# One-hot matrices of the edge tiles on ScalarE instead of VectorE, in a graph network and expert kernel

## The chip, the core and the metric

The kernel runs on one core of a Trainium2 chip. The metric is the device time of one execution in microseconds (us). The core's engines are TensorE (PE in the rows, with PEld for the loading of its weights), VectorE (DVE), ScalarE (ACT), GpSimd (POOL) and SyncE (SP); they run side by side and wait for one another through semaphores. 16 DMA engines move data.

## What is computed

Two layers over 1,250 nodes of 1,024 features. The first is a graph layer with 8 relations and 21,250 edges; the second routes each node to 2 of 8 experts. Only the first matters here, and of it the sum over edges:

```python
u = x @ root + bias
for r in range(8):
    mask = (edge_type == r)
    sums = segment_sum(x[src] * mask[:, None], dst, num_segments=1250)
    cnt = segment_sum(mask, dst, num_segments=1250)
    u = u + (sums / maximum(cnt, 1)[:, None]) @ weight[r]
z = concatenate([u, x], axis=1) @ w_gate + b_gate
h = tanh(u) * z + x * (1 - z)
```

## The kernel before

The kernel first multiplies all nodes by each relation's matrix and stores the results in `Y`. It then takes, for every edge, the row of `Y` that belongs to its source and relation, weighs it by `edge_w` (one over the count), and adds it to its destination. Edges are sorted by destination into 184 tiles of 128 (`ET = 184`), each with destinations in one block of 128 nodes. The change lies in this edge stage.

The edge stage runs beside other products (`x @ root` and half of the gate's product). The generator `steps()` yields 320 "product" steps, of three matmuls each, and 184 "edges" steps, with one or two products between two edge tiles. TensorE, ScalarE and VectorE each walk through the same generator and issue their own part of each step, in that order; an engine's instructions run strictly in the order in which they are written here. "split" and "evacuate" steps belong to the products: halves of the next weights, and results copied from PSUM to `y_out`.

An edge tile t passes through these hands:
- GpSimd gathers 128 rows of `Y` by an indirect DMA into `gathered` (L1053), of which there are 5 buffers (`GR = 5`); it waits until tile t - 5 is used.
- ScalarE writes `ghi`, the row times its weight, rounded (L623, in `edges_hi`). It waits for the gather's landing and, since there are 3 `ghi` buffers (`HR = 3`), until tile t - 3 is used.
- VectorE writes the remainder `glo` (L942, in `edges_lo`), which waits for `ghi`.
- TensorE multiplies `ghi` and `glo` by the tile's one-hot matrix `sel`, four matmuls in all (L1211, L1212, in `edges`), and counts the tile in the semaphore `g_used` (edge_tiles_used).
- Every second tile VectorE adds two PSUM banks to `acc` (L952, in `accumulate`).

`sel` has row e and column d: 1 where edge e of the tile has destination d. It has room for 8 tiles (`SR = 8`) and is written for 4 at a time (`SG = 4`), called a set below: set n is for tiles 4n to 4n + 3. VectorE writes it in one comparison of `iota` (1 to 128) with `edge_dst` (1 to 128, out of that range for a padding edge) in `places` (L935). Sets 0 and 1 are written at the stage's start. Set m + 1 is written behind the work on tile 4m + 2, and may be written once tile 4m - 1 is used, which held its place before.

Of the kernel before, what the change touches and what calls it, by code (L numbers as in the profile page):

```python
# [5 lines left out]
F32 = mybir.dt.float32  # L6
# [4 lines left out]
ALU = mybir.AluOpType  # L11
ACT = mybir.ActivationFunctionType
AX = mybir.AxisListType

P = 128
# [31 lines left out]
def build_program(nc, x, src, dst, edge_type, weight, root, bias, w_gate, b_gate,  # L47
                  gate_w, w1, w2, w3, out):
    s = shapes(x, src, weight, w1, gate_w)
    N, D, R, X, H, NT, NP, KC, HC = (s[k] for k in ("N", "D", "R", "X", "H", "NT", "NP", "KC", "HC"))  # L50
    E, EFULL, EREST, ECOLS, ET, MT, MTE = (
        s[k] for k in ("E", "EFULL", "EREST", "ECOLS", "ET", "MT", "MTE"))
# [6 lines left out]
    with ExitStack() as ctx:  # L59
# [3 lines left out]
        def sem(name):  # L63
            return ctx.enter_context(nc.semaphore(name))
# [29 lines left out]
        iota = keep.put("iota", [P, 257], F32)  # L94
# [4 lines left out]
        edge_dst = keep.put("edge_dst", [P, ET], F32)  # L99
# [14 lines left out]
        R0 = R // 2  # L114
# [62 lines left out]
        tmp10 = z2t.put("tmp10", [P, 4, NT], F32)  # L177

        def x_tile(j):
            return x_first[:, j] if j < XA else x_last[:, j - XA]  # L180

        LN_GROUPS = ((0, 1), (1, 2), (2, 3), (3, 4), (4, 6), (6, 8), (8, NT))
# [5 lines left out]
            sem("ranks_done"), sem("ranks_read"))  # L188
        norm_ready, tr_done, hi_done, lo_done = (
            sem("norm_ready"), sem("transposed"), sem("xhi_written"), sem("xlo_written"))  # L190
        var_ready, sqrt_ready = sem("var_ready"), sem("sqrt_ready")

        groups = [list(range(a, min(a + 3, NT))) for a in range(0, NT, 3)]
        stage = nc.alloc_sbuf_tensor_at("w_stage", [P, 2, 2, HALF], F32, offset=OFF_STAGE)
# [80 lines left out]
        OUTS = 48  # L275
# [6 lines left out]
        row_moved = [sem(f"row_buffer_moved{i}") for i in range(5)]  # L282
# [19 lines left out]
        def w_rows(w, q, h):  # L302
# [5 lines left out]
        GR, HR, SR, SG = 5, 3, 8, 4  # L308
# [5 lines left out]
        sel = Zone(OFF_YOUT + 4 * KB, 4 * KB).put("sel", [P, SR, P], F32R)  # L314
# [7 lines left out]
        sel_ready, g_hi, g_lo, g_used, acc_done = (  # L322
            sem("sel_ready"), sem("rows_hi"), sem("rows_lo"), sem("edge_tiles_used"), sem("pairs_accumulated"))

        def steps():

            a, b = [(NT - 2, k) for k in range(KC)], [(NT - 1, k) for k in range(KC)]
            order = [(j, k) for j in range(NT - 2) for k in range(KC)] + a[:3]
            for k in range(3, KC):
                order += [b[k - 3], a[k]]
            order += b[KC - 3:]
            half, t, later = NT * KC, 0, {}
            for c in range(4 * half):
                g, (j, k) = c // half, order[c % half]
                yield "product", g, j, k

                if (c + 1 - LEAD) * ET // (4 * half - LEAD) > t:
                    yield "edges", t
                    t += 1
                if j == NT - 1 and k % 2 == 1 and g < 3:
                    later.setdefault(c + LAG_SPLIT, []).append(("split", g + 1, k // 2))
                if k == KC - 1:
                    later.setdefault(c + LAG_OUT, []).append(("evacuate", g, j))
                yield from later.pop(c, [])
            for c in sorted(later):
                yield from later[c]  # L350

        with nc.Block() as block:
# [134 lines left out]
            def _(act):  # L487
# [16 lines left out]
                def root_of(g):  # L504
                    a, b = LN_GROUPS[g]
                    act.wait_ge(var_ready, g + 1)
                    nc.scalar.activation(tmp10[:, 1, a:b], tmp10[:, 0, a:b], ACT.Sqrt).then_inc(sqrt_ready, 1)

                def x_hi(j):
                    for n in (2 * j, 2 * j + 1):  # L510
# [99 lines left out]
                def split_hi3(g, q):  # L610
                    act.wait_ge(w_in3[q % 2], 16 * (2 * (g - 1) + q // 2 + 1))

                    if q < 3:
                        act.wait_ge(w_free, 3 * (g - 1) + q + 1)
                    else:
                        act.wait_ge(y_ready3, g * NT)
                    nc.scalar.activation(whi3[:, 2 * q:2 * q + 2, :], stage[:, q % 2], ACT.Copy).then_inc(w_hi3, 1)

                def edges_hi(t):
                    act.wait_ge(g_in[t % GR], G0[t % GR] + 16 * (t // GR + 1))  # L620
                    if t >= HR:
                        act.wait_ge(g_used, t - HR + 1)
                    nc.scalar.activation(ghi[:, t % HR], gath[t % GR][:], ACT.Copy,  # L623
                                         scale=edge_w[:, t:t + 1]).then_inc(g_hi, 1)

                def evacuate3(g, j):
                    act.wait_ge(y_ready3, g * NT + j + 1)
                    if g * NT + j < 2:
                        act.wait_ge(row_moved[j], OUTS * (R - R0))
                    else:  # L630
                        act.wait_ge(y_out3[j % 2], 16 * (g * (NT // 2) + j // 2))
                    nc.scalar.activation(yout[:, j % 2], psum[j % 2][:], ACT.Copy).then_inc(y_evac3, 1)

                for what, *n in steps():
                    if what == "edges":
                        edges_hi(*n)
                    elif what == "split":
                        split_hi3(*n)
                    elif what == "evacuate":
                        evacuate3(*n)  # L640

            @block.vector
            def _(dve):
                v = nc.vector
# [95 lines left out]
                def normalize(g):  # L740
                    a, b = LN_GROUPS[g]
                    for j in range(a, b):
                        dve.wait_ge(xin[j], 16)
                        v.bn_stats(stat[:, j, 0, :], x_tile(j)[:, 0:HALF])
                        step1(v.bn_stats(stat[:, j, 1, :], x_tile(j)[:, HALF:D]))
                        step1(v.bn_aggr(aggr[:, j, :], stat[:, j, :, :].rearrange("p a b -> p (a b)")))
                    v.tensor_scalar(tmp10[:, 0, a:b], aggr[:, a:b, 1], EPS, None, ALU.add).then_inc(var_ready, 1)
                    step1(v.tensor_copy(mean[:, a:b], aggr[:, a:b, 0]))
                    dve.wait_ge(sqrt_ready, g + 1)
                    dve.wait_ge(var_ready, g + 1)  # L750

                    step1(v.reciprocal(tmp10[:, 2, a:b], tmp10[:, 1, a:b]))
                    step1(v.tensor_tensor(tmp10[:, 3, a:b], tmp10[:, 2, a:b], tmp10[:, 2, a:b], ALU.mult))
                    step1(v.tensor_tensor(tmp10[:, 3, a:b], tmp10[:, 3, a:b], tmp10[:, 0, a:b], ALU.mult))
                    step1(v.tensor_scalar(tmp10[:, 3, a:b], tmp10[:, 3, a:b], -0.5, 1.5, ALU.mult, ALU.add))
                    step1(v.tensor_tensor(rstd[:, a:b], tmp10[:, 3, a:b], tmp10[:, 2, a:b], ALU.mult))
                    for j in range(a, b):
                        v.tensor_scalar(x_tile(j), x_tile(j), mean[:, j:j + 1], rstd[:, j:j + 1],
                                        ALU.subtract, ALU.mult).then_inc(norm_ready, 1)
# [163 lines left out]
                v = nc.vector  # L923
# [3 lines left out]
                    v.tensor_tensor(wlo3[:, 2 * q:2 * q + 2, :], stage[:, q % 2],  # L927
                                    whi3[:, 2 * q:2 * q + 2, :].bitcast(F32), ALU.subtract).then_inc(w_lo3, 1)

                def places(n):  # L930

                    if SG * (n + 1) > SR:
                        dve.wait_ge(g_used, SG * (n + 1) - SR)
                    at = SG * n % SR
                    v.tensor_tensor(sel[:, at:at + SG],  # L935
                                    iota[:, 1:P + 1].unsqueeze(1).to_broadcast([P, SG, P]),
                                    edge_dst[:, SG * n:SG * (n + 1)].unsqueeze(2).to_broadcast([P, SG, P]),
                                    ALU.is_equal).then_inc(sel_ready, 1)

                def edges_lo(t):  # L940
                    dve.wait_ge(g_hi, t + 1)
                    v.scalar_tensor_tensor(glo[t % GR][:], gath[t % GR][:], edge_w[:, t:t + 1],  # L942
                                           ghi[:, t % HR].bitcast(F32), ALU.mult, ALU.subtract).then_inc(g_lo, 1)
# [9 lines left out]
                                    ALU.add).then_inc(acc_done, 1)  # L953

                dve.wait_ge(acc_set, NT - 1)
                for i in range(2, 4):
                    dve.wait_ge(row_moved[i], OUTS * (R - R0))
                places(0)
                places(1)
                for what, *n in steps():  # L960
                    if what == "edges":
                        t = n[0]
                        edges_lo(t)

                        if t >= HR and (t - HR) % GROUP == GROUP - 1:
                            accumulate((t - HR) // GROUP)
                        if t % SG == 2 and SR <= t + 2 < ET:
                            places((t + 2) // SG)
                    elif what == "split":
                        split_lo3(*n)  # L970
                for n in range((ET - HR) // GROUP, ET // GROUP):
# [1016 lines left out]
```

## Time and profile before

| | us |
|---|---|
| median of 3 runs | 1840.62 |
| lowest and highest run | 1838.92, 1841.84 |
| the profiled execution's own time | 1834.11 |
| its span, first to last instruction | 1832.4 |
| of it the edge stage, about 889 to 1310 | 421 |

The profile was taken from one further execution. Its times are counted from the span's start. A row's "idle before" is what an engine stood still ahead of the instruction, and the name behind it is what ended that; idle time of an engine that nobody waits for costs nothing.

### The profile page before, as it was taken

Reading aid. Unit: us, or ns where it says so; the run is one execution under the profiler, and the core shown is the slowest. Engines: PE = TensorE matmul, PEld = TensorE weight load, DVE = VectorE, ACT = ScalarE, POOL = GpSimd, SP = SyncE. Lnnn points to the kernel's source line nnn. Section 1 sums busy time; section 2 is a strip of 40 time slices with the busy share of each in tenths; the row PEclk is TensorE's granted clock in tenths of the full one; section 3 lists DMA queues with packets and bytes.
Section 4 is the critical chain, followed back from the end, with each engine's and each line's share of the span. In section 5 each row is a group of like instructions: output and inputs, shape, how many; then the busy total and the mean of one; then the engine's idle time right before and its main releaser. Section 6 shows DMA issues by size and latency. Waiting matters only on the chain. (4 is left out here: it accounts for less than half of the span.)

```text
span 1832.4 us, 22117 instructions
## 1 busy us (share of the span) xinstructions
PE 1708.7 (93%) x7873; PEld 1401.7 (76%) x7873; DVE 1096.1 (60%) x1444; ACT 727.0 (40%) x1230; POOL 749.1 (41%) x663
## 2 busy tenths in 40 slices
PE   7999999999999999999899999989789957999993
PEld 6888888888888888888687777767678846878882
DVE  8555556665464342424399998889799876334200
ACT  2316656631231313121256565556522103454551
POOL 1011222226775656302255545555265515455531
PEclk9999999999999999999899999999899968999997
DMA  5236555566224343434788888888745436877545
GB/s 204 92 121 224 169 176 178 161 193 199 87 92 156 115 152 114 148 127 143 245 281 297 266 283 277 265 290 273 263 170 171 149 115 218 227 186 208 138 88 150
DMA packets 141050, 339.69 MB, mean 185 GB/s; under 512 B 19332, under 2 KB 35764, under 8 KB 140864
## 3 DMA queue, kind: packets, MB, share of 16 engines
q0 software_dynamic: 50816, 159.29, 29.2%
q1 hardware_dynamic: 90128, 179.00, 29.1%
q8 instruction: 66, 1.08, 0.2%
q14 instruction: 40, 0.33, 0.1%
HBM read 241.19 MB, written 102.15 MB: 187 GB/s over the span
## 5 line engine op out<-in xcount | busy, mean ns | idle before, releaser
L1053 POOL DMA_INDIRECT gathered<-Y,edge_row x184 | 211.9, 1152 | 230.2 <-PE banks L1212 191.5
L623 ACT ACTIVATE ghi<-gathered,edge_w 128x1024 fp32r<-128x1024 f32 x184 | 211.7, 1152 | 171.7 <-DMA gathered<-Y,edge_row 162.0
L942 DVE SCALAR_TENSOR_TENSOR glo<-gathered,edge_w,ghi 128x1024 fp32r<-128x1024 f32 x184 | 232.2, 1282 | 48.3 <-ACT ghi L623 47.4
L1029 POOL DMA_INDIRECT edge_w<-INV,edge_key x184 | 207.9, 1130 | 116.8 <-DMA edge_w<-INV,edge_key 85.3
L1070 PE MATMUL banks<-whi,xhi 128*128 128x512 f32 x640 | 253.4, 396 | 0.4 <-DVE xlo L766 0.4
L1072 PE MATMUL banks<-whi,xlo 128*128 128x512 f32 x640 | 250.4, 391 | 0.0
L1071 PE MATMUL banks<-wlo,xhi 128*128 128x512 f32 x640 | 250.2, 391 | 0.0
L1211 PE MATMUL banks<-ghi,sel 128*128 128x512 f32 x368 | 149.0, 405 | 23.8 <-DVE glo L942 23.1
L573 ACT ACTIVATE ring_hi<-raw_chunk 128x512 fp32r<-128x512 f32 x112 | 66.5, 625 | 207.5 <-PE banks L1174 125.6
L1212 PE MATMUL banks<-glo,sel 128*128 128x512 f32 x368 | 144.5, 393 | 0.0
L1072 PEld LDWEIGHTS banks<-whi,xlo 128*128 128x128 f32 x640 | 120.6, 188 | 25.5
L1070 PEld LDWEIGHTS banks<-whi,xhi 128*128 128x128 f32 x640 | 120.9, 189 | 25.0 <-DVE xlo L766 0.8
L1071 PEld LDWEIGHTS banks<-wlo,xhi 128*128 128x128 f32 x640 | 120.9, 189 | 24.1
L1011 POOL DMA_DIRECT2D TW<-t_set x64 | 44.5, 742 | 218.0 <-DVE t_set L676 208.6
L1191 PE MATMUL banks<-whi,xhi 128*128 128x512 f32 x320 | 126.0, 394 | 3.2 <-DVE wlo L911 3.2
L502 ACT ACTIVATE y_out<-banks 128x512 f32<-128x512 f32 x80 | 47.3, 592 | 200.7 <-PE banks L1072 200.3
L1192 PE MATMUL banks<-wlo,xhi 128*128 128x512 f32 x320 | 125.8, 393 | 0.0
L1193 PE MATMUL banks<-whi,xlo 128*128 128x512 f32 x320 | 125.8, 393 | 0.0
L830 DVE TENSOR_TENSOR ring_lo<-raw_chunk,ring_hi 128x512 fp32r<-128x512 f32 x112 | 78.0, 698 | 78.7 <-ACT ring_hi L573 67.2
L1170 PE MATMUL banks<-ring_hi,xhi 128*128 128x512 f32 x320 | 124.6, 389 | 0.0
L1174 PE MATMUL banks<-ring_hi,xlo 128*128 128x512 f32 x320 | 124.6, 389 | 0.0
L1172 PE MATMUL banks<-ring_lo,xhi 128*128 128x512 f32 x320 | 124.6, 389 | 0.0
(316 smaller groups left out, 3677.6 us busy)
## 6 DMA issues: line engine op xcount, KB each, us to landing
raw<-in_L_ffn_w SPq DMA_DIRECT2D x24, 1024.0 KB, 10.2
Y<-y_out SPq DMA_DIRECT2D x80, 256.0 KB
t_set<-in_L_gnn_weight POOLq DMA_DIRECT2D x64, 256.0 KB
TW<-t_set POOLq DMA_DIRECT2D x64, 256.0 KB
raw_chunk<-TW SPq DMA_DIRECT2D x64, 256.0 KB
w_stage<-in_L_gnn_weight SPq DMA_DIRECT2D x30, 512.0 KB, 5.0
raw_chunk<-in_L_gnn_weight SPq DMA_DIRECT2D x48, 256.0 KB
Y<-half_v SPq DMA_DIRECT2D x40, 256.0 KB
```

The lines of the kernel that those rows point to most:

```text
L623: nc.scalar.activation(ghi[:, t % HR], gath[t % GR][:], ACT.Copy, scale=edge_w[:, t:t + 1]).then_inc(g_hi, 1)
L942: v.scalar_tensor_tensor(glo[t % GR][:], gath[t % GR][:], edge_w[:, t:t + 1], ghi[:, t % HR].bitcast(F32), ALU.mult, ALU.subtract).then_in ...
L1029: nc.gpsimd.indirect_dma_start(out=edge_w[:, t:t + 1], out_offset=None, in_=INV, in_offset=bass.IndirectOffsetOnAxis(ap=edge_key[:, t:t + ...
L1053: nc.gpsimd.indirect_dma_start(out=gath[t % GR][:], out_offset=None, in_=Y, in_offset=bass.IndirectOffsetOnAxis(ap=edge_row[:, t:t + 1], a ...
L1070: pe.matmul(psum[slot][:], xhi[:, k, at], whi[h][:, k], start=(k == 0), stop=False)
L1071: pe.matmul(psum[slot][:], xhi[:, k, at], wlo[h][:, k], start=False, stop=False)
L1072: ins = pe.matmul(psum[slot][:], xlo[:, k, at], whi[h][:, k], start=False, stop=(k == KC - 1))
L1191: pe.matmul(psum[j % 2][:], xhi[:, k, at], whi3[:, k], start=(k == 0), stop=False)
L1192: pe.matmul(psum[j % 2][:], xhi[:, k, at], wlo3[:, k], start=False, stop=False)
L1193: ins = pe.matmul(psum[j % 2][:], xlo[:, k, at], whi3[:, k], start=False, stop=(k == KC - 1))
L1211: pe.matmul(bank[:], sel[:, t % SR], ghi[:, t % HR, cols], start=start, stop=False)
L1212: ins = pe.matmul(bank[:], sel[:, t % SR], glo[t % GR][:, cols], start=False, stop=stop)
```

## The change

ScalarE makes `sel` in two passes. The first is `distances(n)`: four activations of 128x128, one a tile, each the absolute value of `edge_dst` less `iota`. `edge_dst` is a column with one value a partition and enters as the activation's bias. The second is `places(n)`: one activation of 128x512 over the whole set, the positive part (Relu) of 1 less the distance, with the 1 read from `iota` as bias. Distances are whole numbers, so the result is 1 at distance 0 and else 0. The semaphore that counted the square roots of the layer norm also counts the distances of a set, so that `places` starts on finished ones.

```diff
+                def distances(n):
+
+                    if SG * (n + 1) > SR:
+                        act.wait_ge(g_used, SG * (n + 1) - SR)
+                    for t in range(SG * n, SG * (n + 1)):
+                        ins = nc.scalar.activation(sel[:, t % SR], iota[:, 1:P + 1], ACT.Abs, scale=-1.0,
+                                                   bias=edge_dst[:, t:t + 1])
+                    ins.then_inc(sqrt_then_distance_ready, 1)
+
+                def places(n):
+                    act.wait_ge(sqrt_then_distance_ready, len(LN_GROUPS) + n + 1)
+                    at = SG * n % SR
+                    nc.scalar.activation(sel[:, at:at + SG], sel[:, at:at + SG].bitcast(F32), ACT.Relu, scale=-1.0,
+                                         bias=iota[:, 1:2]).then_inc(sel_ready, 1)
+
...
+                for i in range(2, 4):
+                    act.wait_ge(row_moved[i], OUTS * (R - R0))
+                distances(0)
+                distances(1)
+                places(0)
+                places(1)
                 for what, *n in steps():
                     if what == "edges":
                         edges_hi(*n)
+                        ahead, part = divmod(n[0] + SR - SG, SG)
+                        if n[0] >= SG and part == 0 and SG * ahead < ET:
+                            distances(ahead)
+                        if n[0] >= SG and part == 1 and SG * ahead < ET:
+                            places(ahead)
...
-                def places(n):
-
-                    if SG * (n + 1) > SR:
-                        dve.wait_ge(g_used, SG * (n + 1) - SR)
-                    at = SG * n % SR
-                    v.tensor_tensor(sel[:, at:at + SG],
-                                    iota[:, 1:P + 1].unsqueeze(1).to_broadcast([P, SG, P]),
-                                    edge_dst[:, SG * n:SG * (n + 1)].unsqueeze(2).to_broadcast([P, SG, P]),
-                                    ALU.is_equal).then_inc(sel_ready, 1)
-
...
                 dve.wait_ge(acc_set, NT - 1)
-                for i in range(2, 4):
-                    dve.wait_ge(row_moved[i], OUTS * (R - R0))
-                places(0)
-                places(1)
                 for what, *n in steps():
...
                         if t >= HR and (t - HR) % GROUP == GROUP - 1:
                             accumulate((t - HR) // GROUP)
-                        if t % SG == 2 and SR <= t + 2 < ET:
-                            places((t + 2) // SG)
```

On ScalarE, from tile 75 to tile 80 of the edge stage, stood before (the first `ghi` is tile 75's, the second tile 76's):

```order
L632 ACTIVATE y_out<-banks 128x512 [waits y3_stored0,y3_ready]
L623 ACTIVATE ghi<-gathered_135,edge_w 128x1024 [waits edge_tiles_used,pool_transfers_landed0]
L623 ACTIVATE ghi<-gathered_136,edge_w 128x1024 [waits edge_tiles_used,pool_transfers_landed1]
L623 ACTIVATE ghi<-gathered_137,edge_w 128x1024 [waits edge_tiles_used,pool_transfers_landed2]
L623 ACTIVATE ghi<-gathered_138,edge_w 128x1024 [waits edge_tiles_used,pool_transfers_landed3]
L632 ACTIVATE y_out<-banks 128x512 [waits y3_stored1,y3_ready]
L623 ACTIVATE ghi<-gathered_139,edge_w 128x1024 [waits edge_tiles_used,pool_transfers_landed4]
L623 ACTIVATE ghi<-gathered_135,edge_w 128x1024 [waits edge_tiles_used,pool_transfers_landed0]
```

In its place stands now, with L631 the distances of set 20, L638 its places and L647 the evacuation:

```order
L647 ACTIVATE y_out<-banks 128x512 [waits y3_stored0,y3_ready]
L623 ACTIVATE ghi<-gathered_135,edge_w 128x1024 [waits edge_tiles_used,pool_transfers_landed0]
L623 ACTIVATE ghi<-gathered_136,edge_w 128x1024 [waits edge_tiles_used,pool_transfers_landed1]
L631 ACTIVATE sel<-iota,edge_dst 128x128 [waits edge_tiles_used]
L631 ACTIVATE sel<-iota,edge_dst 128x128 x3
L623 ACTIVATE ghi<-gathered_137,edge_w 128x1024 [waits edge_tiles_used,pool_transfers_landed2]
L638 ACTIVATE sel<-sel,iota 128x512 [waits sqrt_then_distance_ready]
L623 ACTIVATE ghi<-gathered_138,edge_w 128x1024 [waits edge_tiles_used,pool_transfers_landed3]
L647 ACTIVATE y_out<-banks 128x512 [waits y3_stored1,y3_ready]
L623 ACTIVATE ghi<-gathered_139,edge_w 128x1024 [waits edge_tiles_used,pool_transfers_landed4]
L623 ACTIVATE ghi<-gathered_135,edge_w 128x1024 [waits edge_tiles_used,pool_transfers_landed0]
```

Four distances stand between the `ghi` of tile 76 and that of tile 77, the first with the wait for `g_used`, and the places between those of tiles 77 and 78. So the wait for tile 75 to be used, which VectorE had behind tile 78, ScalarE has behind tile 76.

On VectorE, from tile 78 on, stood before (L942 and `glo` are the remainders, L947 and the ISA rows read the block of the pair and wait, L952 adds):

```order
L942 SCALAR_TENSOR_TENSOR glo_143<-gathered_138,edge_w,ghi 128x1024 [waits rows_hi]
L947 TENSOR_LOAD tile_block
L947 ISA x2
L952 ISA [waits pairs_accumulated,edge_tiles_used]
L952 TENSOR_TENSOR acc<-acc,banks 128x1024
L935 TENSOR_TENSOR sel<-iota,edge_dst 128x512 [waits edge_tiles_used]
L942 SCALAR_TENSOR_TENSOR glo_144<-gathered_139,edge_w,ghi 128x1024 [waits rows_hi]
```

In its place stands now, L942 being L958, L947 L963 and L952 L968:

```order
L958 SCALAR_TENSOR_TENSOR glo_143<-gathered_138,edge_w,ghi 128x1024 [waits rows_hi]
L963 TENSOR_LOAD tile_block
L963 ISA x2
L968 ISA [waits pairs_accumulated,edge_tiles_used]
L968 TENSOR_TENSOR acc<-acc,banks 128x1024
L958 SCALAR_TENSOR_TENSOR glo_144<-gathered_139,edge_w,ghi 128x1024 [waits rows_hi]
```

The comparison between the addition and the remainder of tile 79 is gone; all else stands as it did.

## Rows read from the trace of the kernel before

**Rows 1.** The page's span and its busy times of the engines.
```profile
span 1832.4 us, 22117 instructions
...
PE 1708.7 (93%) x7873; PEld 1401.7 (76%) x7873; DVE 1096.1 (60%) x1444; ACT 727.0 (40%) x1230; POOL 749.1 (41%) x663
```

**Rows 2.** Busy time by stretch: the edge stage, and 50 us of it.
```profile
core 0: us, PE busy (x) PEld busy (x) DVE busy (x) ACT busy (x) POOL busy (x), PEclk, DMA share, GB/s
889.00:1310.00 421.00, 396.44 (x1675) 311.16 (x1674) 371.00 (x334) 241.36 (x236) 211.93 (x184) 0.99 0.85 279
950.00:1000.00 50.00, 47.76 (x200) 36.17 (x198) 46.52 (x43) 31.57 (x32) 25.69 (x23) 1.00 0.89 300
```

**Rows 3.** Who waited for whom, 889 to 1310 us: total, times, longest.
```profile
POOL gathered L1053 <- PE banks L1212: 191.5, 173, 7.1
ACT ghi L623 <- DMA gathered<-Y,edge_row: 162.0, 132, 8.9
...
PE banks L1211 <- DVE glo L942: 23.1, 26, 5.2
ACT ghi L623 <- PE banks L1212: 7.4, 6, 2.6
```

**Rows 4.** Instruction groups by line and form, 889 to 1310 us.
```profile
L942 DVE SCALAR_TENSOR_TENSOR glo<-gathered,edge_w,ghi 128x1024 fp32r<-128x1024 f32 x184 | 232.2, 1282 | 48.3 <-ACT ghi L623 47.4
L935 DVE TENSOR_TENSOR sel<-iota,edge_dst 128x512 fp32r<-128x512 f32 x46 | 31.5, 686 | 1.6 <-DMA Y<-half_u 1.6
```

**Rows 5.** ScalarE's groups by form, whole span.
```profile
L562 ACT ACTIVATE oh_val<-oh_val,val_dst 128x184 fp32r<-128x184 f32 x168 | 73.4, 437 | 41.4 <-DVE oh_val L659 41.4
...
L573 ACT ACTIVATE ring_hi<-raw_chunk 128x512 fp32r<-128x512 f32 x112 | 66.5, 625 | 207.5 <-PE banks L1174 125.6 <-DMA raw_chunk<-TW 36.0 <-issue 25.7
...
L494 ACT ACTIVATE whi<-w_stage 128x1024 fp32r<-128x1024 f32 x30 | 31.6, 1053 | 13.5 <-DMA w_stage<-in_L_gnn_weight 13.5
...
L507 ACT ACT_TABLE_LOAD x1 | 1.3, 1283 | 0.8 <-PEq L1978 0.8
...
L1675 ACT ACTIVATE pr<-lg 128x80 f32<-128x80 f32 x1 | 0.3, 269 | 4.5 <-DVE lg L1752 4.5
```

**Rows 6.** Timeline of ScalarE: activations back to back.
```profile
149.27 0.44 ACT L562 ACTIVATE oh_val<-oh_val,val_dst 128x184 fp32r<-128x184 f32 x1
149.61 0.43 ACT L563 ACTIVATE oh_val<-oh_val,val_src 128x184 fp32r<-128x184 f32 x1
```

**Rows 7.** Timeline, tiles 75 to 77: start, duration, instruction, idle before it.
```profile
1065.28 1.16 ACT L623 ACTIVATE ghi<-gathered,edge_w 128x1024 fp32r<-128x1024 f32 x1 [2.00 <-DMA gathered<-Y,edge_row]
...
1067.77 0.39 PE L1212 MATMUL banks<-glo,sel 128*128 128x512 f32 x1
...
1068.13 1.15 ACT L623 ACTIVATE ghi<-gathered,edge_w 128x1024 fp32r<-128x1024 f32 x1 [1.70 <-DMA gathered<-Y,edge_row]
...
1069.32 1.28 DVE L942 SCALAR_TENSOR_TENSOR glo<-gathered,edge_w,ghi 128x1024 fp32r<-128x1024 f32 x1 [0.22 <-ACT ghi L623]
...
1070.96 0.39 PE L1211 MATMUL banks<-ghi,sel 128*128 128x512 f32 x1
```

**Rows 8.** Timeline: the last matmul of tile 88, and ScalarE's tile 91 behind it.
```profile
1098.99 0.39 PE L1212 MATMUL banks<-glo,sel 128*128 128x512 f32 x1
1099.47 1.15 ACT L623 ACTIVATE ghi<-gathered,edge_w 128x1024 fp32r<-128x1024 f32 x1 [0.25 <-PE banks L1212]
```

**Rows 9.** Timeline of TensorE: tile 3's end, tile 5's start; tile 175's, tile 177's.
```profile
911.51 0.39 PE L1212 MATMUL banks<-glo,sel 128*128 128x512 f32 x1
...
914.99 0.47 PE L1211 MATMUL banks<-ghi,sel 128*128 128x512 f32 x1
...
1292.00 0.40 PE L1212 MATMUL banks<-glo,sel 128*128 128x512 f32 x1
...
1295.88 0.39 PE L1211 MATMUL banks<-ghi,sel 128*128 128x512 f32 x1
```

**Rows 10.** Timeline: the comparison ahead of tile 83's remainder, and tile 83.
```profile
1082.90 0.68 DVE L935 TENSOR_TENSOR sel<-iota,edge_dst 128x512 fp32r<-128x512 f32 x1
...
1083.50 2.48 DVE L942 SCALAR_TENSOR_TENSOR glo<-gathered,edge_w,ghi 128x1024 fp32r<-128x1024 f32 x2
1084.93 0.47 PE L1211 MATMUL banks<-ghi,sel 128*128 128x512 f32 x1 [1.08 <-DVE glo L942]
```

More of the change, by code:

```diff
@@ L190, in build_program @@
             sem("norm_ready"), sem("transposed"), sem("xhi_written"), sem("xlo_written"))
-        var_ready, sqrt_ready = sem("var_ready"), sem("sqrt_ready")
+        var_ready, sqrt_then_distance_ready = sem("var_ready"), sem("sqrt_then_distance_ready")
         groups = [list(range(a, min(a + 3, NT))) for a in range(0, NT, 3)]
@@ L506, in root_of @@
                     act.wait_ge(var_ready, g + 1)
-                    nc.scalar.activation(tmp10[:, 1, a:b], tmp10[:, 0, a:b], ACT.Sqrt).then_inc(sqrt_ready, 1)
+                    nc.scalar.activation(tmp10[:, 1, a:b], tmp10[:, 0, a:b], ACT.Sqrt).then_inc(sqrt_then_distance_ready, 1)
                 def x_hi(j):
@@ L748, in normalize @@
                     step1(v.tensor_copy(mean[:, a:b], aggr[:, a:b, 0]))
-                    dve.wait_ge(sqrt_ready, g + 1)
+                    dve.wait_ge(sqrt_then_distance_ready, g + 1)
                     dve.wait_ge(var_ready, g + 1)
```

## Prediction

> **What bounds the kernel now.** I read the page's busy times first: TensorE is busy 93% of the span, VectorE 60%, ScalarE 40% [rows 1]. That is an average over stages, and the change touches one, so I next cut the span into stretches. In the edge stage, 421 us long, TensorE is busy 396 us, VectorE 371 us and ScalarE 241 us; in the 50 us from 950 on it is 47.8, 46.5 and 31.6 [rows 2]. The reader is to see two nearly full engines and one with a third of its time free. Freeing VectorE and loading ScalarE looks right by these shares.
>
> Shares do not say who is late, so I went to the waits of the stage. TensorE waits 23.1 us in 26 places for `glo`, which VectorE writes. ScalarE waits 162 us for gathered rows to land and hardly for TensorE (7.4 us). GpSimd waits 191.5 us for TensorE to use up a tile, since a gather needs a free buffer [rows 3]. So the stage is a ring: a tile is used, a gather starts, lands, ScalarE, VectorE, TensorE. TensorE sets its pace as long as the ring comes round in time. Whatever ScalarE does later than now goes into the ring, though the engine has 180 us to spare. What matters is the time from a used tile to the next tile's `glo`.
>
> **What is removed.** VectorE loses 46 comparisons of 686 ns, 31.5 us of busy time [rows 4]. Two of them stood at the stage's start. The other 44 stand ahead of the remainder of the tiles 4m + 3. For tile 83 the comparison starts 1082.90, the remainder 1083.50, and TensorE begins the tile at 1084.93 after a wait of 1.08 us for it [rows 10]. Without the comparison the remainder can start 0.60 us earlier, and that wait shrinks to about half. I went through TensorE's timeline for all tiles 4m + 3 and took, from each gap ahead of one, at most the 0.61 us that a comparison holds VectorE. The gaps are 12.8 us in all, and the sum of the parts that can go is 8.4 us. That is the gain.
>
> **What is added, on ScalarE.** No row shows an Abs or a Relu of this shape, so I bound them. A 128x1024 activation without a per-partition operand takes 1053 ns and a 128x512 one 625 ns, so an element costs 0.83 ns and the fixed part is 200 ns; the Exp of 80 columns agrees (269 ns). The one of 184 columns with a per-partition scale takes 437 ns, that is 284 ns fixed [rows 5]. A distance has 128 columns (107 ns) and a per-partition bias: 307 ns by the first kind, 391 ns by the second. I take the second, since its rows too read a column beside the tile. Back to back the 184 column ones start 340 ns apart [rows 6], 97 ns less than their duration, so four distances follow one another at 0.29 us (0.21 us by the cheap price). The places, 128x512, are 0.71 us long and hold the engine 0.61 us. A set so costs ScalarE 4 x 0.29 + 0.61 = 1.8 us, 46 sets 82 us of the 180 that it has free. By shares it fits.
>
> Here a rule speaks against the change. The Trainium skill, on the page "ScalarE: Activation LUTs", section "Rules for kernel authors", says to do relu and simple arithmetic on VectorE and not on ScalarE. The rows agree on engine time (686 ns there against 4 x 391 + 710 ns here, three times as much). If that alone decided, the loss would be 46 times the difference, some 73 us; it does not, since it would be paid in idle time. The rule gives no reason in waits, and the sum below has none of it.
>
> **The wait that comes with it.** The distances of set m + 1 overwrite `sel` of the tiles up to 4m - 1, and ScalarE meets this wait right behind the `ghi` of tile 4m. VectorE met it at tile 4m + 2, when it was over: it had no wait there. ScalarE runs ahead of TensorE by more than that. For m = 19, `ghi` of tile 76 ends at 1066.44, but tile 75 is used only at 1068.16 [rows 7]. So ScalarE stands for 1.7 us (in 42 of the 45 sets it would stand, 1.7 us in the median, by the same reading). What is queued behind are the four distances and then the `ghi` of tile 77, for which VectorE and then TensorE wait.
>
> Now the path from "tile 4m - 1 used" to "TensorE starts tile 4m + 1", step by step:
> - the release takes 0.10 us (tile 88 ends at 1099.38, ScalarE starts at 1099.47) [rows 8];
> - four distances, 4 x 0.29 = 1.17 us;
> - `ghi` 1.15 us, a step of 0.03 us, `glo` 1.28 us [rows 4, 7];
> - from the end of `glo` to TensorE 0.14 us (1083.50 + 1.28 to 1084.93) [rows 10].
>
> Together 3.87 us. TensorE itself covers this distance in 2.80 us at m = 19 (1068.16 to 1070.96) [rows 7]: four matmuls of tile 4m and three products. With four products it is 3.49 us, as at the last set with a wait, 1292.40 to 1295.88; at the first it is 3.09 us (911.90 to 914.99) [rows 9]. So tile 77 starts 1.07 us later than now, and one with four products between 0.38 us later. Where TensorE waited anyway, the distance is longer and the loss smaller. Summed over the 44 sets (half of them stand at about 2.8 us, fourteen at about 3.5, six above 3.87), the loss is 29.3 us. It stays lost, since TensorE is full and has nowhere to catch up. By the cheap price of a distance the path is 3.52 us and the sum 17 us.
>
> The places come behind the `ghi` of 4m + 1 and push that of 4m + 2 back by up to 0.61 us. In the example that one would start at 1071.2 instead of 1070.08, its `glo` would end at about 1073.7, and TensorE, now 1.07 us later, wants it at 1074.3. So I cost the places at nothing; TensorE's own delay hides them. Were it not there, up to 0.6 us a set.
>
> At the stage's start ten activations stand ahead of the first evacuation, about 3.5 us. ScalarE's first `ghi` waits for the first gather, the longest of its waits with 8.9 us [rows 3], and they lie in it. Nothing.
>
> **Sum.** 29.3 - 8.4 = 20.9 us, say 21. Against the profiled execution's 1834.1 us that is 1855; the median of the runs shown is 6.5 us above it, at 1840.6, and there I forecast 1861.6 us, 1.1% slower.
>
> **The rivals.**
> - *The forecast*, slower by 12 to 32 us: the wait and the four distances delay every tile 4m + 1. Chance 0.62.
> - *The cheap one.* The distances cost 0.21 us each, or the gathers land so late that ScalarE has the wait behind it. Then 17 - 8.4 = 9 us, 1850. For it speaks that ScalarE's waits are for landings in 132 of 184 tiles [rows 3]; against it that the bias is a column. Chance 0.16.
> - *The ring closes.* A late tile starts its gather late, and ScalarE's free third, now a sixth, no longer catches up; the gain on VectorE is not had, since ScalarE hands over later everywhere, and the places count at 4m + 2. Then 29.3 + 44 x 0.3 = 42 us, 1883. It decides once landings are later than ScalarE is ready; the page shows DMA busy 0.85 of the stage [rows 2]. Chance 0.08.
> - *Faster.* VectorE is the true bound, at 93% of the 50 us stretch [rows 2]. All 17.9 us of TensorE's waits for `glo` behind the first (23.1 less 5.2) [rows 3] go, the new wait being met by chance in tiles where TensorE has four products. It decides if the path above is under 2.8 us, that is if a distance takes under 0.03 us or ScalarE is not ahead. The best is 1840.6 - 17.9 = 1823, more likely 1834. Chance 0.07.
> - *No change.* Gain and loss cancel: a path of 3.2 us instead of 3.87. Chance 0.06.
> - *Table loads.* If Abs, Relu and Copy did not share a table, each of two switches a set would cost a load of 1.28 us [rows 5], at least 100 us in all. The built program has no load there, the two that it has being those of the square root and of tanh. The Trainium skill, same page, section "Table sets: the hidden batching unit", has these cheap functions in every set, which would leave none to load. Chance 0.01.
>
> **How the numbers follow.** A measurement of this kernel can tell about 0.2%, 3.7 us. The time is that of the forecast, 1861.6. The range leaves out 0.07 below for the faster, a few hundredths of no change, and the closed ring above: 1845 to 1877, which holds the cheap price and the sum without any gain (1870). Slower is 0.62 + 0.16 + 0.08 + 0.01, faster 0.07, within 0.2% 0.06.
>
> **What the profile would show.** The wait: ScalarE's distances (L631) idle for TensorE's L1212, some 60 to 75 us in some 40 places. The prices: a distance about 390 ns, the places about 710 ns. The loss: TensorE's waits for `glo` grow from 23 us to above 40 us, and sit at tiles 4m + 1. The gain: hardly any at 4m + 3. The stage grows from 421 to about 442 us, and nothing before or behind it changes. It is wrong if the waits on L631 are short, if the distances are much cheaper, or if TensorE's waits stay at 23 us or fall.

## The result, and the profile after

The changed kernel takes 1864.15 us (median of 5, 1860.76 to 1867.57) against 1838.92 us (median of 5) before: ratio 1.0138, 95% interval 1.0121 to 1.0155. It is 25 us slower. A second set of 5 beside other kernels (e8 below) gave 1.0136 (1.0110 to 1.0161). Of the five executions of e8 and of e10, one each took over 4,400 us; these two count in the medians given below, but not in the ratios. The forecast was 21 us.

The span of its profiled execution grew from 1832.4 us [rows 1] to 1862.9 us. These 30.5 us are a pair of single executions, of which that of before lies below its median. The page:

```profile
span 1862.9 us, 22302 instructions
...
PE 1721.4 (92%) x7873; PEld 1404.1 (75%) x7873; DVE 1071.4 (58%) x1398; ACT 799.8 (43%) x1460; POOL 755.9 (41%) x663
```

Busy time by stretch, columns as in [rows 2]. The edge stage now ends near 1340 us, 30 us later than before; nothing ahead of it moved.

```profile
889.00:1340.00 451.00, 405.18 (x1675) 310.86 (x1673) 345.67 (x288) 313.88 (x466) 219.04 (x184) 0.98 0.81 260
```

VectorE does 25 us less than in [rows 2] and ScalarE 73 us more. TensorE and VectorE are idle for longer than before, and ScalarE still for 137 us. No engine became full, and yet the stage is longer. The waits of the stage (889 to 1342 or 1345 us) say why; columns: total, times, longest.

```profile
POOL gathered L1063 <- PE banks L1222: 214.4, 175, 6.2
ACT sel L631 <- PE banks L1222: 107.1, 43, 4.2
DVE glo L958 <- ACT ghi L623: 99.5, 90, 12.5
PE banks L1221 <- DVE glo L958: 45.3, 57, 3.8
PEld banks L1221 <- ACT sel L638: 43.4, 32, 2.3
...
ACT ghi L623 <- DMA gathered<-Y,edge_row: 19.6, 23, 5.5
```

Against [rows 3] the second row is new: ScalarE stands 107 us for a used tile, in 43 places. Its wait for landings fell from 162 to 20 us, since rows land while it stands or is late. TensorE's wait for `glo` doubled. The PEld row looks like a wait for the places, and is not one: the set that they write is first used by tile 4m + 4, and in the example below TensorE starts tile 77 0.15 us after its `glo` ends (1082.53 + 1.28), 0.85 us after the places are over (1082.40 + 0.71). ScalarE's groups by form:

```profile
L631 ACT ACTIVATE sel<-iota,edge_dst 128x128 fp32r<-128x128 f32 x184 | 58.8, 391 | 111.1 <-PE banks L1222 107.1 <-DMA Y<-half_u 4.0
L638 ACT ACTIVATE sel<-sel,iota 128x512 fp32r<-128x512 f32 x46 | 32.5, 708 | 0.0
```

A distance takes 0.39 us and the places 0.71 us. The tiles of [rows 7], 75 to 77, on the timeline of the changed kernel:

```profile
1079.74 0.39 PE L1222 MATMUL banks<-glo,sel 128*128 128x512 f32 x1
...
1080.17 1.28 ACT L631 ACTIVATE sel<-iota,edge_dst 128x128 fp32r<-128x128 f32 x4 [2.19 <-PE banks L1222]
...
1081.35 1.14 ACT L623 ACTIVATE ghi<-gathered,edge_w 128x1024 fp32r<-128x1024 f32 x1
...
1082.40 0.71 ACT L638 ACTIVATE sel<-sel,iota 128x512 fp32r<-128x512 f32 x1
1082.53 1.28 DVE L958 SCALAR_TENSOR_TENSOR glo<-gathered,edge_w,ghi 128x1024 fp32r<-128x1024 f32 x1 [1.37 <-ACT ghi L623]
...
1083.01 1.13 ACT L623 ACTIVATE ghi<-gathered,edge_w 128x1024 fp32r<-128x1024 f32 x1
1083.96 0.47 PE L1221 MATMUL banks<-ghi,sel 128*128 128x512 f32 x1 [0.88 <-DVE glo L958]
```

This is the predicted path in one piece. The last matmul of tile 75 is over at 1080.13 (1079.74 + 0.39), and ScalarE, idle for 2.19 us, starts its four distances at 1080.17. Then come the `ghi` of tile 77 (1081.35), its `glo` (1082.53, with VectorE idle for 1.37 us ahead of it) and its matmul (1083.96, after 0.88 us in which TensorE waited). From used tile to matmul it is 3.83 us.

To see where TensorE stands still, I took from its timeline, for each edge tile from 4 on, the time between the start of its first matmul and the start of the matmul before, less the usual 0.227 us, and summed it in us by the tile's place in its set. "Stage" is from the first edge matmul to the end of the last. The experiments' rows are there too.

| kernel | 4m | 4m + 1 | 4m + 2 | 4m + 3 | stage, us |
|---|---|---|---|---|---|
| before | 2.8 | 8.3 | 1.9 | 12.8 | 407.0 |
| after | 2.8 | 40.9 | 2.6 | 5.3 | 437.8 |
| steps later (e1) | 5.0 | 11.9 | 2.8 | 4.5 | 406.8 |
| room for 12 (e2) | 2.4 | 11.1 | 5.0 | 8.0 | 408.4 |
| wait alone (e3) | 2.8 | 9.5 | 1.3 | 14.4 | 410.2 |
| no sel (e4) | 3.0 | 11.7 | 4.4 | 6.6 | 405.7 |
| one distance (e5) | 5.4 | 12.4 | 2.4 | 5.8 | 407.9 |
| eight distances (e6) | 0.7 | 93.2 | 3.3 | 2.9 | 500.1 |
| no places (e7) | 3.4 | 41.3 | 2.6 | 3.4 | 433.9 |
| the change again (e8) | 2.8 | 40.9 | 3.4 | 5.9 | 439.3 |
| no places, again (e9) | 3.8 | 42.1 | 2.7 | 2.4 | 435.0 |
| places later (e10) | 4.0 | 43.1 | 1.4 | 3.4 | 433.1 |

After the change TensorE stands ahead of all 44 tiles 4m + 1 with distances ahead of them (11 before), 32.6 us more in all, and 7.5 us less ahead of the tiles 4m + 3.

### The profile page after: what moved, and what is told of

Read it like the earlier page. It is cut to its first block and busy times, and to the rows that moved or that the text cites. A ratio compares the mean times of both kernels' runs of the same rounds, so it can differ in the third digit from the quotient of the medians.

```text
span 1862.9 us, 22302 instructions
## 1 busy us (share of the span) xinstructions
PE 1721.4 (92%) x7873; PEld 1404.1 (75%) x7873; DVE 1071.4 (58%) x1398; ACT 799.8 (43%) x1460; POOL 755.9 (41%) x663
## 5 line engine op out<-in xcount | busy, mean ns | idle before, releaser
L1063 POOL DMA_INDIRECT gathered<-Y,edge_row x184 | 219.0, 1190 | 253.4 <-PE banks L1222 214.4
L958 DVE SCALAR_TENSOR_TENSOR glo<-gathered,edge_w,ghi 128x1024 fp32r<-128x1024 f32 x184 | 232.7, 1282 | 99.6 <-ACT ghi L623 99.5
L623 ACT ACTIVATE ghi<-gathered,edge_w 128x1024 fp32r<-128x1024 f32 x184 | 206.4, 1141 | 24.3 <-DMA gathered<-Y,edge_row 19.6
L1221 PEld LDWEIGHTS banks<-ghi,sel 128*128 128x128 f32 x368 | 69.6, 189 | 88.6 <-ACT sel L638 43.4
```

What stands on the lines that cost most here:

```text
L1063: nc.gpsimd.indirect_dma_start(out=gath[t % GR][:], out_offset=None, in_=Y, in_offset=bass.IndirectOffsetOnAxis(ap=edge_row[:, t:t + 1], a ...
L1221: pe.matmul(bank[:], sel[:, t % SR], ghi[:, t % HR, cols], start=start, stop=False)
```

## The experiments

Gaps and stages in the table come from one profiled execution of each kernel, the ratios below from the timed runs. The first four experiments separate the wait from the work. The path theory, that of the forecast, says that the loss is the wait for tile 4m - 1 plus the four distances, ahead of tile 4m + 1. The rivals are the engine-time one (ScalarE cannot carry the extra work) and the wait-alone one.

**e1, the same work two steps later.**

```diff
-                        if n[0] >= SG and part == 0 and SG * ahead < ET:
+                        if n[0] >= SG and part == 2 and SG * ahead < ET:
                             distances(ahead)
-                        if n[0] >= SG and part == 1 and SG * ahead < ET:
+                        if n[0] >= SG and part == 3 and SG * ahead < ET:
                             places(ahead)
```

> The changed kernel with the distances of a set behind the first part of tile 4m + 2 and the places behind that of 4m + 3, same instructions, two steps later. There the wait for tile 4m - 1 is one that ScalarE has already passed. Path theory (the loss is the wait for tile 4m - 1 and four distances ahead of tile 4m + 1): the loss goes and the gain on VectorE stays, so 3 to 8 us faster than before, ratio 0.996 to 0.998. Engine-time rival (82 us more work is what ScalarE cannot carry, wherever it stands): stays 20 us or more slower, ratio near 1.012. Wait-alone rival (the wait is all of it): as the path theory.

Measured: 1835.03 us, ratio 0.9969 (0.9956 to 0.9983). The same instructions in the same number on the same engine, and the loss has become a gain of 5.7 us. ScalarE's groups in the stage:

```profile
L623 ACT ACTIVATE ghi<-gathered,edge_w 128x1024 fp32r<-128x1024 f32 x184 | 210.5, 1148 | 97.4 <-DMA gathered<-Y,edge_row 91.7 <-PE banks L1222 4.2
L631 ACT ACTIVATE sel<-iota,edge_dst 128x128 fp32r<-128x128 f32 x184 | 58.1, 387 | 4.0 <-DMA Y<-half_u 4.0
```

The distances are as dear as in the changed kernel and wait for nothing but the stage's start. The engine-time rival falls.

**e2, the same work in the same place, with room for 12 tiles.** The wait is there, but for a tile used long ago.

```diff
-        GR, HR, SR, SG = 5, 3, 8, 4
+        GR, HR, SR, SG = 5, 3, 12, 4
...
-        sel = Zone(OFF_YOUT + 4 * KB, 4 * KB).put("sel", [P, SR, P], F32R)
+        sel = [nc.alloc_sbuf_tensor_at(f"sel{i}", [P, SG, P], F32R, offset=o)
+               for i, o in enumerate((OFF_YOUT + 4 * KB, OFF_YOUT + 6 * KB, after_acc))]
...
-                        ahead, part = divmod(n[0] + SR - SG, SG)
+                        ahead, part = divmod(n[0] + SG, SG)
...
```

Left out here are the places where `sel` is read or written, which now name the set's buffer and the tile's place in it.

> The changed kernel with room for 12 tiles of sel in place of 8 (the third set in a spare 2 KB), the distances and places where the change has them, behind tiles 4m and 4m + 1. The wait is now for tile 4m - 5 and is over when ScalarE meets it. Path theory: without the wait the four distances, 1.2 us, lie in the 1.7 us by which ScalarE is ahead at tile 4m, so within 4 us of before on either side, ratio 0.997 to 1.002. Engine-time rival: near 1.012 still. Wait-alone rival: 0.996 to 0.998 as in the late one.

Measured: 1834.95 us, 0.9967 (0.9955 to 0.9980). The distances stand exactly where the change has them, between the `ghi` of 4m and of 4m + 1, and cost nothing. This is as fast as e1, just below the path theory's range of 0.997 to 1.002 and inside the wait-alone rival's. So the distances alone are harmless, and e3 has to tell the two theories apart.

**e3, the wait without the work.**

```diff
                     if what == "edges":
                         edges_hi(*n)
+                        if n[0] >= SG and n[0] % SG == 0 and n[0] + SG < ET:
+                            act.wait_ge(g_used, n[0])
```

> The kernel before, VectorE comparing as it did, and on ScalarE behind tile 4m only the wait for tile 4m - 1 to be used, without any distance or places. Path theory: from the used tile to the start of 4m + 1 the path is then 2.70 us against 2.80 us that TensorE needs, so nearly nothing: 0 to 5 us slower, ratio 1.000 to 1.003. Wait-alone rival: 20 us or more slower, ratio above 1.010. Engine-time rival: 1.000.

Measured: 1841.01 us, 1.0010 (1.0000 to 1.0020), that is 0 to 4 us slower. The waits of the stage:

```profile
ACT ghi L623 <- DMA gathered<-Y,edge_row: 115.6, 96, 8.8
DVE glo L944 <- ACT ghi L623: 49.1, 68, 9.4
...
ACT ghi L623 <- PE banks L1214: 43.4, 27, 3.3
...
PE banks L1213 <- DVE glo L944: 24.4, 33, 4.7
```

ScalarE stands 43 us for TensorE against 7 in [rows 3], and TensorE's own wait is 24.4 us against 23.1. Most of the standing still is free. The wait-alone rival falls. With e2 the finding is that the wait alone costs 4 us at most and the distances alone nothing that can be told. Behind one another they make the path longer than TensorE's distance.

**e4, the relief of VectorE by itself.** The sets from 2 on are left out, and nobody makes them.

```diff
-                        if t % SG == 2 and SR <= t + 2 < ET:
-                            places((t + 2) // SG)
...
-                    pe.wait_ge(sel_ready, t // SG + 1)
+                    pe.wait_ge(sel_ready, min(t // SG, 1) + 1)
```

> The kernel before without the comparisons of sets 2 to 45 on VectorE and nothing in their place: these sets are left out, and TensorE uses the first two over and over. It gives the worth of the relief by itself. By the sum of the prediction 8.4 us faster, ratio 0.9954; if VectorE were the bound of the stage, 18 to 30 us faster, ratio 0.984 to 0.990.

Measured: 1836.31 us, 0.9976 (0.9965 to 0.9987): 4.4 us faster, half of the 8.4 us, and far from 18. The table shows where gains went: the gaps at 4m + 3 fall from 12.8 to 6.6 us, and those at the other three places grow from 13.0 to 19.1 us. In this pair of single executions all of it comes back; by the timed runs, half. The waits of this kernel:

```profile
POOL gathered L1051 <- PE banks L1210: 188.7, 169, 6.9
ACT ghi L623 <- DMA gathered<-Y,edge_row: 162.4, 124, 8.9
...
PE banks L1209 <- DVE glo L942: 23.2, 26, 4.3
```

TensorE waits for `glo` as long as before, and ScalarE for landings as well. Followed back through `glo` and `ghi`, TensorE's gaps of over 0.1 us were in the kernel before 7.4 us for a comparison (20 tiles) and 8.3 us for a gather that landed late (12 tiles). In e4 the first part is gone, and late landings make 14.4 us (20 tiles). The largest other part, a split of weights ahead of `glo`, went from 7.8 to 6.5 us. So the wait that came back is mostly for the gathers. That a faster gather would give it back was not tested.

The next three vary the length of the path and what is behind it.

**e5, one distance a set.** The other three are left out from set 2 on.

```diff
-                    for t in range(SG * n, SG * (n + 1)):
+                    for t in range(SG * n, SG * (n + 1) if n < 2 else SG * n + 1):
```

> The changed kernel, wait and places kept where they are, but from set 2 on only the first of the four distances of a set; the other three are left out. Path theory: the path falls from 3.83 us (as measured in the changed kernel) by 3 x 0.29 to 2.95 us, 0.15 us above what TensorE needs in half of the sets, so with the gain on VectorE kept: 3 us faster to 4 us slower than before, ratio 0.998 to 1.002. Engine-time rival: 38 us of 91 us of ScalarE's work go, so the loss shrinks by about 40%, to 1.008. Wait-alone rival: near 1.012.

Measured: 1839.57 us, 1.0007 (0.9991 to 1.0023). Wait and places are as in the changed kernel, and its loss is gone, as the path theory had it (0.998 to 1.002). The engine-time rival, at 1.008, and the wait-alone one, near 1.012, are both outside the interval.

```profile
ACT sel L631 <- PE banks L1222: 76.5, 41, 3.2
...
PE banks L1221 <- DVE glo L958: 24.0, 27, 6.7
```

ScalarE stands 76 us here without harm. The wait's total says little; what counts is what is still to be done behind it.

**e6, eight distances a set.**

```diff
+                    for t in range(SG * n, SG * (n + 1) if n >= 2 else SG * n):
+                        nc.scalar.activation(spare[:, t % SG], iota[:, 1:P + 1], ACT.Abs, scale=-1.0,
+                                             bias=edge_dst[:, t:t + 1])
                     for t in range(SG * n, SG * (n + 1)):
```

> The changed kernel with four more distances of the same size, into a spare buffer, ahead of the four of each set from set 2 on. Path theory: the path grows by 1.17 us, and TensorE waits already in all 44 sets, so nearly all of 44 x 1.17 = 51 us is paid: 45 to 55 us on top of the change, ratio to before 1.038 to 1.045. Wait-alone rival: little on top, 1.014 to 1.020. Engine-time rival: between, 1.02 to 1.03, as there were still 130 us of idle ScalarE.

Measured: 1926.30 us, 1.0472 (1.0455 to 1.0488), 62 us on top of the change. That is far above both rivals, and above the path theory's own 45 to 55 us. The gaps at 4m + 1 grow from 40.9 to 93.2 us. That is 52.3 us for 44 x 1.17 = 51.5 us of work, so it is paid in full. The stage grew by more, 62.3 us, while the gaps at all four places grew by 48.5 us. The other 14 us I had not expected. Busy time by stretch of this kernel, with the granted clock third from the end:

```profile
889.00:1402.00 513.00, 417.04 (x1672) 321.94 (x1670) 344.96 (x287) 363.75 (x642) 192.58 (x184) 0.95 0.72 229
```

The clock is 0.95 against 0.99 in [rows 2]; the last section comes back to it. ScalarE is busy 364 of 513 us, 71%, in the slowest of all these kernels.

**e7 and e9, no places.** The second pass is left out from set 2 on, and the distances serve as `sel`.

```diff
+                    if n < 2:
-                    nc.scalar.activation(sel[:, at:at + SG], sel[:, at:at + SG].bitcast(F32), ACT.Relu, scale=-1.0,
-                                         bias=iota[:, 1:2]).then_inc(sel_ready, 1)
+                        nc.scalar.activation(sel[:, at:at + SG], sel[:, at:at + SG].bitcast(F32), ACT.Relu, scale=-1.0,
+                                             bias=iota[:, 1:2]).then_inc(sel_ready, 1)
+                    else:
+                        act.sem_inc(sel_ready, 1)
```

> The changed kernel without the second pass, the places, from set 2 on (the distances themselves serve as sel); everything else as it is. Prediction's step: the places are hidden behind TensorE's own delay, so within 3 us of the changed kernel, ratio to before 1.012 to 1.014. If they were part of the loss through tile 4m + 2, up to 44 x 0.3 = 13 us less, ratio near 1.007.

Measured: 1858.46 us, 1.0107 (1.0090 to 1.0124), between the two expectations. The next three are the changed kernel (e8) and this one (e9) side by side, and with them a kernel with the places moved (e10).

**e8, the changed kernel again.**

> The changed kernel once more, so that the two beside it are compared with it on the same chip. 1.012 to 1.0155 of before.

Measured: 1866.65 us, 1.0136 (1.0110 to 1.0161).

> The changed kernel without the places from set 2 on, again, beside the changed kernel. If they are hidden, as predicted, the two differ by under 3 us. If they count (the earlier runs, on another chip run, gave 1.0107 and 1.0138), this one is 4 to 8 us faster than the changed kernel.

Measured: 1860.29 us, 1.0107 (1.0085 to 1.0128). Two pairs agree on 0.0029 to 0.0031, some 5.5 us. The intervals against the kernel before overlap, but side by side e9's slowest execution (1864.57 us) is hardly above the fastest of e8 (1864.38 us). So the places are likely not free, and not dear.

**e10, the places behind 4m + 3.**

```diff
-                        if n[0] >= SG and part == 1 and SG * ahead < ET:
+                        if n[0] >= SG and part == 3 and SG * ahead < ET:
                             places(ahead)
```

> The changed kernel with the places of a set behind the first part of tile 4m + 3 in place of 4m + 1; the distances and their wait stay behind tile 4m. If the places count because they stand ahead of the first part of 4m + 2, while ScalarE is late from the distances, this takes their cost away as leaving them out does: 4 to 8 us faster than the changed kernel, ratio to before 1.009 to 1.011. If it is their engine time, nothing changes, 1.013. The path theory has it at 1.009 or above either way, as the wait and the distances still stand ahead of 4m + 1; should it come near the late one, 0.997, the theory falls.

Measured: 1863.04 us, 1.0123 (1.0097 to 1.0149). It lies between "nothing changes" and "their cost goes", and its interval holds both, so the times do not say whether the 5.5 us come from the place or from the engine time. The traces point to the place. I took the time from the matmul before a tile to the tile's last one, less four times 0.227 us, and summed it over the tiles 4m + 2 and 4m + 3. It is 11.2 and 12.5 us in the two profiles of the changed kernel, 7.0 and 6.7 us without places (e7, e9), and 5.7 us in e10, where ScalarE does all the work of the change. These are single executions. The path theory's part held: with the wait and distances ahead of 4m + 1 the loss stays.

## Why the prediction was right, and where its sizes were off

- **The direction, the place and the mechanism were right.** The wait that VectorE had already passed at 4m + 2 is a real one for ScalarE at 4m. e1 and e2 take it away by order and by room, and both turn 25 us slower into 6 us faster.
- **The prices were right.** 391 and 710 ns were forecast from a row with a per-partition operand and 391 and 708 ns measured. The cheap price, 307 ns, was wrong.
- **The path was right.** 3.87 us forecast, 3.83 us measured; 34 of the 44 sets lie within 0.03 us of that.
- **The loss was a little too small.** 29.3 us forecast, 32.6 us measured at the tiles 4m + 1. The term that was missing is ScalarE's other work. The forecast's steps have nothing between the distances and the next `ghi`, but in nine sets an evacuation (six times, 0.48 us each) or a split of weights (three times, 1.04 us each) stands there, as at tile 85 (L617):

```profile
1099.69 1.28 ACT L631 ACTIVATE sel<-iota,edge_dst 128x128 fp32r<-128x128 f32 x4 [3.00 <-PE banks L1222]
1100.88 1.04 ACT L617 ACTIVATE whi<-w_stage 128x1024 fp32r<-128x1024 f32 x1
1101.83 1.14 ACT L623 ACTIVATE ghi<-gathered,edge_w 128x1024 fp32r<-128x1024 f32 x1
```

The path is 4.3 us long in five of these sets, 4.87 us in three and 5.95 us in one, where ScalarE itself reached its distances 1.7 us after the used tile. In numbers: the measured path of 3.83 us, set against TensorE's distances of the trace before as the forecast did, gives 27.8 us. The nine sets and a tenth of 4.13 us at the stage's start add 6.8 us. In four sets TensorE's wait of before was longer than the one that replaced it, which takes 2.0 us off.
- **The gain was too large.** 8.4 us forecast, 7.5 us seen at 4m + 3 in the changed kernel, but 4.4 us (2.4 to 6.4, from the interval of e4) when it stands alone. With ScalarE's work in place but out of the path, e1 and e2 gained 5.7 and 6.1 us (intervals together 3 to 8 us), so the whole 8.4 us was seen nowhere. The step "that is the gain" took the gaps one by one. In this ring, part of the wait that went in one place came back in another, mostly for the gathers.
- **The places were reckoned at nothing** and cost some 5 us by two pairs of runs. That step ("TensorE's own delay hides them") failed, on this evidence. By the traces of e7, e9 and e10 the cost sits at the tiles 4m + 2 and 4m + 3 and comes from where the places stand; the timed runs of e10 alone do not settle it.
- **No luck in the number.** The three misses on the sum (loss too small, gain too large, places at nothing) all lie on the same side, so they did not cancel: 21 us forecast, 25 us measured.
- **ScalarE's wait was too short.** 60 to 75 us forecast, 107 us measured. In the changed kernel ScalarE ends the `ghi` of 4m a median of 2.4 us ahead of the used tile, not 1.7. This changed nothing, as the path starts at the used tile; e5 has 76 us of it for free. The forecast also read 45 sets, of which 44 carry the wait.
- **The rule on the engine.** In engine time it holds: 4 x 391 + 708 ns on ScalarE (0.39 and 0.71 us in the rows above) stand for 686 ns on VectorE [rows 4]. The Trainium skill, "ScalarE: Activation LUTs", section "Rules for kernel authors", prefers VectorE for relu and simple arithmetic. Taken alone that rule would speak against e1 and e2 too, and they are 0.3% faster than before: with VectorE busy for 88% of the stage (371 of 421 us) and ScalarE for 57%, and no wait added, the dearer form on ScalarE wins here. The measurement decides.
- **The rivals.** "Faster" needed a path under 2.8 us, "no change" one of 3.2 us. e5, whose shortest path is 2.95 us, lies between them, and it is not told from before. "The ring closes" (1883 us) did not come about: late landings make 1.0 us of TensorE's gaps in the changed kernel, against 8.3 us before.

By the table the gaps account for 25.8 of the 30.8 us by which the profiled stage grew. Of the other 5 us some 3 lie in two stretches of a lower clock, below, and 2 within the edge tiles: behind a wait a tile's second matmul starts a little later than 0.23 us after the first, as at 1114.06 and 1114.36 below.

## What to carry to other kernels

When work moves to an idle engine, its waits move too, and they land at another point of that engine's order. Ask which wait is passed at that point, and sum the work from the release to the consumer, not the engine's busy share. Here the same 1.8 us a set cost 25 us at one point of ScalarE's order and gained 6 us two steps later, or with one more buffer at the same point.

A gain read from gaps one by one in a ring of buffers is best taken as an upper bound: here a quarter to a half of it was not had. And when a path through an engine is summed, the whole order of that engine counts, also the work that stands there only in some rounds.

Two runs (room for the wait, no work behind it) told more than the busy shares. ScalarE is busy for 57% of the stage before, 70% in the changed kernel and 75% in e1, one of the two fastest:

```profile
889.00:1311.00 422.00, 397.12 (x1674) 312.35 (x1672) 347.65 (x288) 317.73 (x466) 217.66 (x184) 0.99 0.84 279
```

## What else the runs showed

Stretches of a lower clock are more frequent where TensorE waits much. In the changed kernel TensorE waits 1.96 us ahead of tile 88:

```profile
1111.70 0.40 PE L1203 MATMUL banks<-whi,xlo 128*128 128x512 f32 x1
1114.06 0.47 PE L1221 MATMUL banks<-ghi,sel 128*128 128x512 f32 x1 [1.96 <-DVE glo L958]
1114.36 0.39 PE L1222 MATMUL banks<-glo,sel 128*128 128x512 f32 x1
...
1115.22 0.63 PE L1201 MATMUL banks<-whi,xhi 128*128 128x512 f32 x1
1115.65 0.63 PE L1202 MATMUL banks<-wlo,xhi 128*128 128x512 f32 x1
...
1118.39 0.40 PE L1201 MATMUL banks<-whi,xhi 128*128 128x512 f32 x1
1118.63 0.40 PE L1202 MATMUL banks<-wlo,xhi 128*128 128x512 f32 x1
```

From about 1114.8 to 1118.2 us the granted clock is at the lower of its two levels, 1.2 GHz, and matmuls start 0.43 us apart in place of 0.23. Such a stretch of 3.4 us costs up to (3.4 / 0.43) x 0.20 = 1.6 us. From 909 us on, 20 us into the stage, the kernel before has none, the changed one has two in each of its two profiles, e1 has one, and e6, with 93 us of gaps at 4m + 1, has twelve. Ten more than in the changed kernel are 16 us at most, which is the size of the 14 us that e6's gaps left open. But e10, with as long gaps as the changed kernel (51.9 us in all, against 51.6), has none. So the sum of the waits does not settle it. That the waits bring the stretches about is read from their company; no run tested it by itself.
